# Attention probabilities laid out block-diagonally: four ScalarE block copies onto a tile zeroed once, in place of four masked products

## The reference

```
x  = x + attn(cond(x))                    # cond: einsum('bct,bcd->bdt', x, w[subjects])
x  = x + ffn(cond2(x))                    # cond2: x @ W.T plus top-2 gated low-rank experts

attn: q, k, v = x@wq.T, x@wk.T, x@wv.T    # 32 heads of 16; rotary embedding on q and k
      scores  = q @ k.T / sqrt(16), causal within a sequence of 32
      attn    = softmax(scores)
      out     = (attn @ v) @ wo.T
ffn:  permute columns, per head of 32: up to 128, gelu, down to 32, permute back
```

## Time and profile before

| | us |
|---|---|
| median of 3 runs | 310.91 |
| lowest and highest | 307.98, 311.3 |
| span of the profiled execution, first to last instruction | 309.0 |
| busy in it: PE, DVE, POOL, ACT | 262.6, 228.2, 123.9, 101.6 |

### The profile page before, as it was taken

One profiled execution on the slowest core, in us unless ns is written; L12 is line 12 of the kernel. 1 busy time (PEld: TensorE's weight loads), 2 busy tenths in 40 slices (PEclk: granted clock), 3 DMA queues, 4 the chain that ended last, 5 costly groups with the idle time before them and its releaser, 6 DMA issues.

```text
span 309.0 us, 5764 instructions
## 1 busy us (share of the span) xinstructions
PE 262.6 (85%) x2288; PEld 211.3 (68%) x2288; DVE 228.2 (74%) x450; ACT 101.6 (33%) x180; POOL 123.9 (40%) x97
## 2 busy tenths in 40 slices
PE   0789589997858989997989989997798799788895
PEld 0679476795636778776767878786586686557873
DVE  1654399899996888999936978799656888854502
ACT  1332561421212244821202246620211347521360
POOL 2728368786560531463740805236805313200000
PEclk9869989999798999999979999999899999999999
DMA  5599421000000000002100000001000000001001
GB/s 144 162 349 216 88 86 52 0 2 0 2 1 1 3 2 0 2 2 91 47 0 1 2 0 2 2 0 70 0 1 2 0 2 3 0 2 69 0 2 68
DMA packets 13498, 11.42 MB, mean 37 GB/s; under 512 B 7576, under 2 KB 9368, under 8 KB 13472
## 3 DMA queue, kind: packets, MB, share of 16 engines
q1 hardware_dynamic: 12608, 9.85, 10.6%
q0 software_dynamic: 576, 1.18, 1.3%
q10 hardware_dynamic: 288, 0.03, 0.1%
HBM read 8.96 MB, written 2.10 MB: 36 GB/s over the span
## 4 chain that ended last, share of the span: by engine, by line
DVE 42%; PE 36%; issue 7%; DMA 5%; SPq 4%; ACT 4%; POOL 1%; DVEq 0%; ACTq 0%
DVE pbd L1088 13%; PE ps_D L439 5%; SPq L321 4%; PE ps_D L441 4%; PE ps_D L440 4%; PE ps_C L439 3%; PE ps_C L441 3%; DVE rot L1030 3%; PE ps_C L440 3%; DVE kbd L1041 3%; DVE small L1135 2%; PE ps_S L614 2%; PE ps_A L439 2%; DMA pbd<-in_L_ffn_perm 2%; PE ps_S L503 2%
## 5 line engine op out<-in xcount | busy, mean ns | idle before, releaser
L1088 DVE TENSOR_SCALAR pbd<-pr,cst 128x256 f32<-128x256 f32 x96 | 53.7, 618 | 0.6 <-PE ps_C L518 0.4
L386 POOL TENSOR_TENSOR kbd<-kr,cst 128x1024 f32<-128x1024 f32 x16 | 31.7, 1993 | 39.7 <-PE ps_S L503 39.7
L373 POOL TENSOR_TENSOR rot<-rot,cst 128x512 f32<-128x512 f32 x16 | 20.7, 1291 | 39.2 <-DVE rot L1030 39.1
L396 POOL TENSOR_TENSOR pr<-pr,small 128x512 f32<-128x512 f32 x16 | 21.6, 1348 | 36.9 <-DVE small L1060 36.9
L860 ACT ACTIVATE pbd<-pr,cst 128x256 f32<-128x256 f32 x32 | 15.5, 504 | 53.3 <-PE ps_C L518 26.7
L518 PE MATMUL ps_C<-pbd,vz 128*32 128x128 f32 x512 | 20.5, 280 | 13.1 <-DVE pbd L1088 12.7
L518 PEld LDWEIGHTS ps_C<-pbd,vz 128*32 128x32 f32 x512 | 12.4, 109 | 21.4 <-DVE pbd L1088 13.4
L873 ACT ACTIVATE act<-ps_D 128x512 f32<-128x512 f32 x32 | 19.1, 598 | 12.9 <-PE ps_D L441 11.3
L439 PE MATMUL ps_A<-xc,wkT 128*128 128x256 f32 x64 | 19.2, 300 | 4.3 <-DVE qr L1031 4.3
L1041 DVE TENSOR_TENSOR kbd<-kr,cst 128x1024 f32<-128x1024 f32 x16 | 22.5, 1428 | 0.0
L403 POOL TENSOR_TENSOR pr<-pr,small 128x512 f32<-128x512 f32 x16 | 16.7, 1062 | 12.1 <-DVE small L1071 12.1
(11 more groups left out here) (183 smaller groups left out, 745.7 us busy)
## 6 DMA issues: line engine op xcount, KB each, us to landing
xs<-in_x SPq DMA_DIRECT2D x4, 512.0 KB, 4.7
out<-xs SPq DMA_DIRECT2D x3, 512.0 KB, 2.8
pbd<-in_L_attn_wq SPq DMA_DIRECT2D x2, 512.0 KB, 6.5
act<-in_L_attn_wk SPq DMA_DIRECT2D x1, 1024.0 KB, 5.6
pr<-in_L_attn_wv SPq DMA_DIRECT2D x1, 1024.0 KB, 9.4
xs<-in_L_attn_wo SPq DMA_DIRECT2D x1, 1024.0 KB, 11.7
out<-xs SPq DMA_DIRECT2D x2, 256.0 KB, 2.0
pbd<-in_L_cond_A SPq DMA_DIRECT2D x1, 256.0 KB
```

What stands on the lines that cost most here:

```text
L373: pool.tensor_tensor(rv, rv, con("sin").unsqueeze(1).to_broadcast([P, 2 * N // T, T]), ALU.mult).then_inc(rot_sin, 1)
L386: pool.tensor_tensor(kbd[:, c, :, :].rearrange("p b (h s) -> p b h s", h=HC), kv.unsqueeze(2).to_broadcast([P, BT, HC, T]), con("head").un ...
L396: pool.tensor_tensor(pr[:, i, :, :], pr[:, i, :, :], mx[:, i, :].unsqueeze(2).to_broadcast([P, NH // 2, T]), ALU.subtract).then_inc(shifte ...
L1088: i = ve.tensor_scalar(pbd[:, c % 2, :, b, :], src, con("seq")[:, b:b + 1], None, ALU.mult)
```

## The change

The tile `pbd` is set to zero once by GpSimd, after the raw weights in it have been read, and from then on only the four diagonal blocks of a chunk are written, by four ScalarE copies of 32 partitions by 256 elements each. VectorE's three products a chunk are gone, and with them `probs_blocks` and the semaphore `pbd_v`.

```
@@ gpsimd, between k_blocks(0, 0, 3) and the loop over groups
+            wait_full(pool, prep("r"))
+            pool.wait_ge(bs_ready, 1)
+            pool.wait_ge(pick_ready, KC)
+            pool.memset(pbd[:, :, :, :, :], 0.0).then_inc(pbd_zero, 1)
             for g in range(G):
                 k_blocks(g, 1, 1)
@@ tensor, pv
-                pe.wait_ge(pbd_v, n + 1)
                 pe.wait_ge(pbd_a, n + 1)
@@ scalar, probs_block
                 if n == 0:
-                    wait_prep(sc, "r", 1)
-                src = pT(2 * t + c // 2)[:, HC * (c % 2):HC * (c % 2) + HC, :]
-                b = BT - 1
-                sc.activation(pbd[:, c % 2, :, b, :], src, ACT.Copy, scale=con("seq")[:, b:b + 1]
-                              ).then_inc(pbd_a, 1)
+                    sc.wait_ge(pbd_zero, 1)
+                for b in range(BT):
+                    at = slice(T * b, T * b + T)
+                    last = copy(pbd[at, c % 2, :, b, :], pT(2 * t + c // 2)[at, HC * (c % 2):HC * (c % 2) + HC, :])
+                last.then_inc(pbd_a, 1)
@@ vector
-            def probs_blocks(g, t, c):
-                n = 8 * g + 4 * t + c
-                ve.wait_ge(turned, 4 * g + 2 * t + c // 2 + 1)
-                if n >= 2:
-                    wait_pv(ve, n - 2)
-                ...
-                for b in range(BT - 1):
-                    i = ve.tensor_scalar(pbd[:, c % 2, :, b, :], src, con("seq")[:, b:b + 1], None, ALU.mult)
-                i.then_inc(pbd_v, 1)
@@ vector, in the order of each group: all eight calls of probs_blocks go, nothing else moves
```

More of the change, by code:

```diff
@@ L279, in build @@
         summed, recip, normed, turned = sem("summed"), sem("recip"), sem("normed"), sem("turned")
-        pbd_v, pbd_a, pv_done = sem("pbd_v"), sem("pbd_a"), sem("pv_done")
+        pbd_zero, pbd_a, pv_done = sem("pbd_zero"), sem("pbd_a"), sem("pv_done")
         o_hi = sem("o_hi")
@@ L1077, in turn @@
                 ve.transpose(pT(i), pr[:, i, :, :]).then_inc(turned, 1)
-            def probs_blocks(g, t, c):
-                n = 8 * g + 4 * t + c
-                ve.wait_ge(turned, 4 * g + 2 * t + c // 2 + 1)
-                if n >= 2:
-                    wait_pv(ve, n - 2)
-                if n == 0:
-                    wait_prep(ve, "r", 1)
-                src = pT(2 * t + c // 2)[:, HC * (c % 2):HC * (c % 2) + HC, :]
-                for b in range(BT - 1):
-                    i = ve.tensor_scalar(pbd[:, c % 2, :, b, :], src, con("seq")[:, b:b + 1], None, ALU.mult)
-                i.then_inc(pbd_v, 1)
             def o_lo(g, t):
@@ L1246, in _ @@
                     turn(g, 0)
-                    probs_blocks(g, 0, 0)
-                    probs_blocks(g, 0, 1)
                     rope(1, 1)
@@ L1252, in _ @@
                     sums(g, 3)
-                    probs_blocks(g, 0, 2)
                     rope(1, 2)
-                    probs_blocks(g, 0, 3)
                     turn(g, 2)
                     turn(g, 3)
-                    probs_blocks(g, 1, 0)
                     rope(1, 3)
                     o_lo(g, 0)
-                    probs_blocks(g, 1, 1)
                     blocks(2)
-                    probs_blocks(g, 1, 2)
-                    probs_blocks(g, 1, 3)
                     for j in range(4):
```

## The result

The changed kernel takes 298.5 us, the median of 4 runs (295.57 to 299.18), against 309.45 of the kernel before beside it (307.68 to 311.3): ratio 0.9615, interval 0.9563 to 0.9667. The profiled execution has a span of 296.7 us, against 309.0. The forecast was 296.6, its range 291 to 303.

What follows compares the result with a forecast made beforehand. It took TensorE's waits for VectorE's masked products to bound the kernel. Group 0 -7.9, groups 1 and 2 -10.3, group 3 +3.9 gave -14.3 us on a span of 309.0: 294.7, or 296.6 as run median, range 291 to 303.

Steps and rivals of the forecast that it cites:

- What bounds the kernel: TensorE, held up by VectorE's masked products before `pv`: 12.7 us in 8 waits, from a full queue and GpSimd beside it.
- Part 1, groups 1 and 2: Removing VectorE's products gives TensorE 3.7 us of waits and 1.45 of slow clock per group: 5.15 each, -10.3 together.
- Parts 1 and 2, group 0: Waits and slow clock of 10.15 us go, less 1.6 for the memset and 0.7 for a late `add_x`: -7.9.
- Part 3, the copy: One ScalarE block copy takes 422 ns, between 384 and 508.
- the open question: How closely a chunk's four ScalarE copies follow each other: 1.4 us with overlap, 1.7 without, 1.55 taken.
- Part 3, group 3: Without projections between chunks ScalarE's copies aren't hidden: group 3 loses 2.3 to 5.4 us, middle 3.9.
- The sum: -7.9 - 10.3 + 3.9 = -14.3 us on the span of 309.0, thus 294.7, or 296.6 in the runs' terms.
- The first rival: Clock stays low in groups 0 to 2 although the waits are gone: 5.8 us, giving 302.4; chance 0.12.
- In group 3 `pv` waits for ScalarE in every chunk: Expected sign in group 3: TensorE's `pv` waits for ScalarE's copies in every chunk.
- No window at 0.50 after 70 us: Expected sign: after 70 us the granted clock never stands at 0.50 of 2.4 GHz.
- None over 0.5 us for ScalarE in groups 0 to 2: Expected sign: in groups 0 to 2 no `pv` waits over 0.5 us for ScalarE.
- The rule against the change: Skill advice to use VectorE, not ScalarE, for multiplications; rows agreed where GpSimd is quiet (306 against 494 ns), not beside it (1997).

Runs made afterwards that it cites:

- e8: Kernel before plus one wait: GpSimd's `kbd` for the next group held until VectorE's last product of this group; 299.98 us, ratio 0.966.
- e4: Changed kernel's memset and block copies, but VectorE writes three of four blocks as in the kernel before; 313.68 us, ratio 1.0143.
- e1: Changed kernel without memset or block copies: ScalarE does all four products over 128 partitions with the scale column; 294.51 us, ratio 0.9538.
- e3: Changed kernel, but in group 3 alone VectorE copies three blocks of a chunk and ScalarE the fourth; 294.04 us, ratio 0.9533.
- e6: Kernel before, with ScalarE doing all four 128-partition products in groups 0 to 2, group 3 split as before; 289.63 us, ratio 0.933.
- e9: e5 plus 18 unused matmuls filling TensorE's wait ahead of group 3's transposes of the gates; 289.8 us, ratio 0.9344.
- e10: e6 plus the same 18 unused matmuls as e9; 289.03 us, ratio 0.931.
- e2: Changed kernel with the memset moved behind GpSimd's second `kbd` for tile 1 of group 0; 296.02 us, ratio 0.9581.
- e5: Changed kernel with the diffs of e2 and e3 together: late memset and shared group 3; 290.62 us, ratio 0.9355.
- e7: Changed kernel with the memset done twice in a row at its place; 300.91 us, ratio 0.9684.

## Why the prediction was right, and where it was off

- **What bounds the kernel** held. The waits of `pv` on VectorE were the price (12.7 us), GpSimd's `kbd` beside VectorE was about half of it (e8), and the block form had no part in the gain (e4 slower, e1 faster than the change). The prediction put the slowing on the two `kbd` instructions alone; GpSimd's `rope` instructions do it too (three products 2.65 us against 0.84). GPSIMD Engine Reference (the Trainium skill, section Key points), which the prediction cited for the shared SBUF interfaces, gives no price there; here `kbd` beside the products costs the 3.4% of e8.
- **Part 1, groups 1 and 2**: forecast -5.15 each, measured -5.67 and -5.55. All the waits named are gone, no new one came. The 0.4 to 0.5 more lie beside the same waits: from `pv(1,2)` to `wo_proj` 3.25 us became 1.01, which is 0.2 more than the wait of 2.04, and `pv(1,0)` comes 1.84 us earlier in its group, 0.2 more than its wait of 1.65.
- **Parts 1 and 2, group 0**: forecast -7.9 with the memset in it, measured -7.20. The memset's length was right (1.84 against 1.81 us) and so was the place where it bites: a wait of 2.32 us before `scores(0,3)`, forecast 1 to 2. Its cost in the scores was 2.47 in place of 1.6 to 1.7, and the rest of group 0 gave 9.67 in place of 9.45. The idle 3.29 us ahead of the memset were in the forecast: 0.92 of them stood there before, and the other 2.4 are the forecast's way from 52.42 to 54.8. What it had wrong are the two `shift`s behind the `kbd`, put at 2.1 us together; they took 3.03, since VectorE's `kbd` (2.68 us from 55.05) stood beside the first of them after all. Timeline of GpSimd in the changed kernel, against the earlier trace rows:

```profile
52.97 1.81 POOL L414 MEMSET pbd<- 128x2048 f32 x1 [3.29 <-PE ps_C L668]
54.74 1.90 POOL L386 TENSOR_TENSOR kbd<-kr,cst 128x1024 f32<-128x1024 f32 x1
56.61 3.03 POOL L396 TENSOR_TENSOR pr<-pr,small 128x512 f32<-128x512 f32 x2
59.60 1.90 POOL L386 TENSOR_TENSOR kbd<-kr,cst 128x1024 f32<-128x1024 f32 x1
```

- **Part 3, the copy**: 422 ns forecast, 415 measured; the open question, how closely four follow, went to the upper bound, 1.7 us a chunk (the forecast took 1.55). The estimate of 399 ns from ScalarE: Activation LUTs (the Trainium skill, section What ACT_TABLE_LOAD costs) is near the trace's 414; its overlap of 93 ns back to back agrees with the products (0.498 long, 0.42 apart, thus 0.08 of overlap) and not with copies that change their group of 32 partitions (0.414 long, 0.43 apart). For those the trace agrees with what VectorE: DVE Perf Modes (the Trainium skill, section Two Vector instructions with no wait between them) says of VectorE.
- **Part 3, group 3**: this is the term that was mis-sized most. Forecast +3.9 (2.3 to 5.4), measured +7.94. ScalarE's copies made 3.73 + 0.46 = 4.2 of it, as forecast (0.2 of that is clock too, in `unpermute`); the other 3.8 are the low clock, 2.13 in `wo_proj` and 1.65 behind the wait for the gates. The sum had the low clock as a cost that vanishes in groups 0 to 2 and never as one that new or old waits of group 3 could bring. The first rival had this mechanism, but in groups 0 to 2, where it didn't happen.
- **"In group 3 `pv` waits for ScalarE in every chunk"**: five of eight chunks do. "No window at 0.50 after 70 us" was wrong, by the same term. "None over 0.5 us for ScalarE in groups 0 to 2" holds (one of 0.2).
- **The sum**: -14.3 forecast on the span. The terms measured give -7.2 - 11.2 + 7.9 = -10.5, and -1.8 of the start, which was not in the sum, makes the -12.3 of the two spans. The ratio of the runs, 0.9615, is worth 11.9 us. That the time of 298.5 us came within 0.7% of the forecast is partly luck: the kernel before took 309.45 us beside it and not the 310.91 from which the forecast was counted, and of the gain of 14.3 us 11.9 came, with the loss of group 3 at twice its forecast.
- **The rule against the change** (VectorE, not ScalarE, for multiplications; ScalarE: Activation LUTs, the Trainium skill, section Rules for kernel authors) would have kept the slower kernel: e1 breaks it outright and is 4.6% faster. In group 3, where GpSimd is quiet, it was better to give VectorE three of four blocks (e3, e6), as the rule says; that two engines then share the work may count as much, and no run tells these apart.

What stays open is what decides whether a wait brings the clock down. The wait for the gates (2.2 to 2.3 us) is alike in all of these kernels but e9 and e10, and in the profiled executions the clock fell behind it in the changed kernel, e1, e2, e3 and e5, and not in the kernel before, e4, e6, e7 and e8. In e7 it fell behind the waits for ScalarE alone, and for longer (244 to 259 us), so that its group 3 took 86.6 us all the same. The wait of 1.8 us ahead of `wo_proj` is alike in the eight kernels that share group 3, and the low clock followed it in e3, e4 and e8 and not in the other five.

## What to carry to other kernels

When an instruction's longest case is several times its median, look at which other engine runs then, and move or delay one of the two before making the instruction smaller: a quarter of the partitions was worth nothing here, another engine 4.6%, and one wait 3.4%. Look at all that the other engine does then: its short instructions slowed the products as well as its long ones. Decide the engine per stage, not per kernel: the move paid where projections hid it and VectorE stood beside GpSimd, and cost 4.2 us in the last group, where neither was so. In a sum, price every wait that is left or made with the low clock that may follow it, not only those that vanish.

## What the runs showed of the hardware that was not expected

- Four ScalarE copies of 32 partitions each, on successive groups of 32, don't overlap (0.414 us long, 0.43 apart), while four of 128 partitions do (0.498 long, 0.42 apart): four copies of a quarter of the partitions take ScalarE as long as four products of all of them.
- A VectorE copy of 32 partitions beside GpSimd's `kbd` takes as long as a product of 128: 1906 against 1997 ns at worst, and one `kbd` of GpSimd takes 1.94 us. Three products take 0.84 us alone, 2.65 beside GpSimd's `rope` instructions of 1.3 us each, and 4.31 with its `kbd` behind these.
- The same wait of TensorE of about 2 us was followed by 3 to 4 us at 1.2 GHz in five of the profiled executions and by none in five others; it cost 1.65 us in the changed kernel. With the wait filled group 3 was 1.45 us shorter in one profiled execution of each (e9 against e5), which the times of the runs don't confirm.
